# Routing weights broadcast to 128 partitions from SBUF rows instead of from HBM, with four transposes instead of one

## The reference

```python
x = x + 0.5 * ffn(layernorm(x), ...)
x = x + mixer(layernorm(x), ...)     # gated convolution and linear recurrence
x = x + 0.5 * ffn(layernorm(x), ...)
```

```python
scores = sigmoid(tokens @ router_weight.T)
# the best 2 of 4 groups of experts, of these the best 4 experts
topk_w = scores of the chosen / their sum * 2.5
hidden = silu(tokens @ gate_w[e].T) * (tokens @ up_w[e].T)
mixed  = sum over the chosen e of topk_w[e] * (hidden @ down_w[e].T)
shared = (silu(tokens @ shared_gate.T) * (tokens @ shared_up.T)) @ shared_down.T
```

## Time and profile before

| | |
|---|---|
| median of 3 runs | 724.22 us (724.0 to 727.43) |
| profiled execution, its own time | 724.26 us |
| its span in the profile | 722.5 us |
| TensorE busy | 668.6 us (93%) |
| VectorE busy | 580.9 us (80%) |
| GpSimd busy | 480.9 us (67%) |
| ScalarE busy | 420.2 us (58%) |
| DMA moved | 78.84 MB |

### The profile page before, as it was taken

One profiled execution on the slowest core, in us unless ns is written; L12 is line 12 of the kernel. 1 busy time (PEld: TensorE's weight loads), 2 busy tenths in 40 slices (PEclk: granted clock), 3 DMA queues, 4 the chain that ended last, 5 costly groups with the idle time before them and its releaser, 6 DMA issues. The chain is left out here.

```text
span 722.5 us, 10391 instructions
## 1 busy us (share of the span) xinstructions
PE 668.6 (93%) x3016; PEld 524.4 (73%) x3016; DVE 580.9 (80%) x1543; ACT 420.2 (58%) x801; POOL 480.9 (67%) x714
## 2 busy tenths in 40 slices
PE   6589998988987999999999999999999899999996
PEld 5468776776766887767777787776778677777784
DVE  5787797788978788887897969988788887978663
ACT  4446655664665656566566565655665655665553
POOL 1147657765677766777567775777667776686775
PEclk9899999999999999999999999999999999999999
DMA  8492908308373290925719074461907346190550
GB/s 196 99 205 70 198 1 191 62 5 194 70 168 75 57 216 4 198 55 113 154 46 192 15 178 89 105 133 45 216 7 167 85 99 139 41 196 16 126 128 15
DMA packets 59994, 78.84 MB, mean 109 GB/s; under 512 B 7680, under 2 KB 27168, under 8 KB 59936
## 3 DMA queue, kind: packets, MB, share of 16 engines
q1 hardware_dynamic: 59408, 77.91, 49.8%
q10 hardware_dynamic: 528, 0.26, 0.2%
HBM read 75.01 MB, written 3.15 MB: 108 GB/s over the span
## 5 line engine op out<-in xcount | busy, mean ns | idle before, releaser
L479 POOL TENSOR_TENSOR hid_lo<-hid,hid_hi 128x256 fp32r<-128x256 f32 x544 | 392.1, 743 | 200.7 <-ACT hid_hi L576 200.0
L576 ACT ACTIVATE hid_hi<-hid 128x512 fp32r<-128x512 f32 x272 | 170.5, 627 | 118.5 <-DVE hid L725 117.3
L712 DVE TENSOR_TENSOR weighted<-gate_ps,raw 128x512 f32<-128x512 f32 x256 | 175.4, 685 | 68.7 <-ACT gate_ps L568 55.8
L568 ACT ACTIVATE gate_ps<-gate_ps 128x512 f32<-128x512 f32 x256 | 148.6, 580 | 105.5 <-PE gate_ps L982 103.0
L725 DVE TENSOR_TENSOR hid<-weighted,up_ps 128x512 f32<-128x512 f32 x256 | 174.8, 683 | 13.8 <-DVE weighted L712 0.5
L1025 PE MATMUL down_ps<-hid_hi,wt_hi 128*128 128x512 f32 x272 | 108.7, 400 | 6.7 <-ACT ffn_sb L580 6.7
L1028 PE MATMUL down_ps<-hid_lo,wt_hi 128*128 128x512 f32 x272 | 108.2, 398 | 0.8 <-POOL hid_lo L479 0.7
L1026 PE MATMUL down_ps<-hid_hi,wt_lo 128*128 128x512 f32 x272 | 107.9, 397 | 0.0
L980 PE MATMUL up_ps<-xT_hi,wt_hi 128*128 128x512 f32 x187 | 78.1, 417 | 12.5 <-DVE hid L725 12.2
L980 PE MATMUL gate_ps<-xT_hi,wt_hi 128*128 128x512 f32 x187 | 80.6, 431 | 4.1 <-DVE weighted L712 3.9
L982 PE MATMUL gate_ps<-xT_hi,wt_lo 128*128 128x512 f32 x187 | 74.8, 400 | 0.0
(11 more groups left out here) (140 smaller groups left out, 1082.7 us busy)
## 6 DMA issues: line engine op xcount, KB each, us to landing
raw<-wT_hbm SPq DMA_DIRECT2D x64, 640.0 KB, 13.3
raw<-wT_hbm SPq DMA_DIRECT2D x32, 512.0 KB, 7.7
raw<-wT_hbm SPq DMA_DIRECT2D x32, 256.0 KB, 3.9
x_res<-in_L_attn_x SPq DMA_DIRECT2D x8, 256.0 KB, 5.6
out_x<-x SPq DMA_DIRECT2D x8, 256.0 KB, 2.3
x_ln<-in_L_attn_x SPq DMA_DIRECT2D x7, 256.0 KB, 14.1
raw<-in_L_ffn_gate_w SPq DMA_DIRECT2D x4, 256.0 KB, 5.3
raw<-in_L_ffn_up_w SPq DMA_DIRECT2D x4, 256.0 KB, 4.9
```

Of the source, the lines that this page charges most:

```text
L479: last = nc.gpsimd.tensor_tensor(hid_lo[s][:, cols], hid[s][:, cols], hid_hi[s][:, cols].bitcast(F32), ALU.subtract)
L568: nc.scalar.activation(bank[:, :] if j else silu_sb[:, :], bank[:, :], ACT.Silu).then_inc(silu_done, 1)
L576: nc.scalar.activation(hid_hi[s][:, :], hid[s][:, :], ACT.Copy).then_inc(hid_hi_done, 1)
L712: V.tensor_tensor(weighted[j % 2][:, :], gate_ps[n % BANKS][:, :], wb[:, j - 1, :], ALU.mult)\
```

## The change

The store to HBM and its buffer and semaphore are gone. The transposed weights stay in SBUF in another form: `wT` is now [32, 512], one partition for each expert with its 512 weights in a row, and there are two such buffers, used by turns. To get this form, `w_tok` is laid out as tokens by experts, and TensorE makes four transposes, one for each 128 tokens, each giving 32 x 128; ScalarE then copies 32 x 512. SyncE broadcasts each expert's row from its one partition to the 64 partitions of that expert with a transfer of its own: 32 transfers of 128 KB a unit, in the same four chunks with the same waits. The bytes written to `wb` are the same.

```diff
-        wT_hbm = nc.dram_tensor("wT_hbm", [E, BLK], F32, kind="Internal").ap()
-        w_tok = sb("w_tok", [P, E, TT])
-        wT = {k: sb(f"wT{k}", [P, P]) for k in (1, 4)}
+        w_tok = sb("w_tok", [P, TT, E])
+        wT = [sb("wT0", [E, BLK]), sb("wT1", [E, BLK])]
...
                 else:
-                    for loaded in wb_loaded:
-                        sp.wait_ge(loaded, u * 32)
-                sp.dma_start(wT_hbm.rearrange("e (t p) -> (e t) p", t=TT), wT[k][:, :]).then_inc(wT_stored, 16)
-                sp.wait_ge(wT_stored, u * 16 + 16)
+                    for loaded, (lo, hi) in zip(wb_loaded, CHUNKS):
+                        sp.wait_ge(loaded, u * 32 * (hi - lo))
                 for c, (lo, hi) in enumerate(CHUNKS):
                     if u > 0:
                         sp.wait_ge(weighted_done, (u - 1) * NPAIR + hi)
-                    for half in range(2):
-                        rows = wT_hbm.rearrange("(q h) t -> h q t", h=2)[half, lo:hi, :]
-                        sp.dma_start(wb[half * I:half * I + I, lo:hi, :], rows.partition_broadcast(I))\
-                          .then_inc(wb_loaded[c], 16)
+                    for q in range(lo, hi):
+                        for half in range(2):
+                            row = wT[u % 2][2 * q + half:2 * q + half + 1, :]
+                            sp.dma_start(wb[half * I:half * I + I, q, :], row.unsqueeze(1).broadcast_to([1, I, BLK]))\
+                              .then_inc(wb_loaded[c], 16)
...
-                if u > 0:
-                    act.wait_ge(wT_stored, u * 16)
-                nc.scalar.activation(wT[k][:, :], side[:, 0:P], ACT.Copy).then_inc(wT_done[k], 1)
+                if u > 1:
+                    for loaded, (lo, hi) in zip(wb_loaded, CHUNKS):
+                        act.wait_ge(loaded, (u - 1) * 32 * (hi - lo))
+                nc.scalar.activation(wT[u % 2][:, :], side[0:E, :], ACT.Copy).then_inc(wT_done[k], 1)
...
-                dve.wait_ge(wb_loaded[chunk_of(j - 1)], n // NT * 32 + 32)
+                lo, hi = CHUNKS[chunk_of(j - 1)]
+                dve.wait_ge(wb_loaded[chunk_of(j - 1)], (n // NT + 1) * 32 * (hi - lo))
...
-                    st.done(V.scalar_tensor_tensor(w_tok[:, :, :].rearrange("p e t -> p t e"), chosen[:, :, 0:E], SCALE,
+                    st.done(V.scalar_tensor_tensor(w_tok[:, :, :], chosen[:, :, 0:E], SCALE,
...
-                nc.tensor.transpose(side[:, 0:P], w_tok[:, :, :].rearrange("p e t -> p (e t)"), ident[:, :])\
-                  .then_inc(route_transposed[k], 1)
+                for t in range(TT):
+                    last = nc.tensor.transpose(side[0:E, t * P:(t + 1) * P], w_tok[:, t, :], ident[:, :])
+                last.then_inc(route_transposed[k], 1)
```

More of the change, by code:

```diff
@@ L231, in macaron_kernel @@
         w_lo_done = sem("w_lo_done")
-        wT_stored = sem("wT_stored")
         wb_loaded = [sem(f"wb_loaded{c}") for c in range(len(CHUNKS))]
```

## The result

The changed kernel takes 2191.95 us (median of 4 runs, 2191.88 to 2192.03) where the kernel before took 725.03 us beside it: 3.023 times as long, 95% interval 3.017 to 3.028.

What follows compares the result with a forecast made beforehand. TensorE bounds the kernel before; after the change the broadcasts would. First issue 30.5, transfers 1741, gaps 35, late weights 35, x loads about 10, end 27, outside the span 1.8: together 1880 us, range 721 to 2700.

Steps and rivals of the forecast that it cites:

- places of eight neighbouring partitions: SBUF source of the broadcasts: eight partitions share one rate, 218/8 = 27.3 GB/s, so 4.80 us a transfer with all engines there.
- 16 x 32 x 3.40 = 1741: Broadcast time in us: 16 units of 32 transfers at 3.40 us, geometric middle between one place (4.80) and two (2.40).
- nothing holds the engines together within a unit: DMA engines in the broadcasts: one ahead finds the next place free and gets further ahead, so 3.40 us, not 4.80.
- Gaps of 2.3: SyncE between units: one landing and one issue, 2.3 us, 15 times, 35 us.
- Late weights 35: Three units with weights at slots 13, 16 and 14 wait 2, 5 and 3 tiles of some 3.5 us, 35 us.
- The end from the last landing, 27: After the last broadcast lands: five tiles at 3.4 us (17), then 10.3 us from last weighting to end; 27 us.
- The transposes and the removed store: Three transposes more a unit cost TensorE about 5 us in all; dropping the store gains about 5 us; they cancel.
- The signs I named: Profile after: DMA 30 to 50 GB/s, share near 1; TensorE under 45%; VectorE's broadcast wait longest, over 50 us a unit.
- Everything stands at one place: Rival for the broadcasts: engines stay in step at one place, 4.80 us a transfer, 2600 us; chance 0.17.
- No slower than HBM: Rival for the broadcasts: reading one partition costs nothing extra, only small terms count, 719 to 729 us; chance 0.22.
- The engines spread widely: Rival for the broadcasts: three to eight places at work, 1.6 to 0.6 us a transfer, 728 to 1300 us; chance 0.14.
- Slower than a place of eight: Rival for the broadcasts: a single partition gives 13.6 GB/s without spreading, about 5070 us, anything over 2700; chance 0.06.

Runs made afterwards that it cites:

- e4: Kernel before, with its eight broadcasts a unit cut into 32 of one row each, still from HBM: 724.41 us, ratio 0.9987.
- e1: Changed kernel with all transfers reading partition 0, the row of expert 0: 2567.48 us.
- e9: Changed kernel with transfers reading partitions 0 and 4 by turns: 1374.79 us.
- e10: Changed kernel with transfers reading partitions 0 and 2 by turns: 2567.66 us.
- e5: Changed kernel's layout, four transposes and 512-column copy, but with the store to HBM and eight broadcasts of the kernel before: 729.11 us, ratio 1.0052.
- e3: Changed kernel with rows laid out so that eight consecutive transfers read eight different groups of four partitions: 1160.74 us.
- e6: Changed kernel with rows laid out so that four consecutive transfers read four different groups of four partitions, the fifth the first again: 1085.70 us.

## Why the prediction was right

*Direction and mechanism.* I forecast 1880 us with a range of 721 to 2700, and 2192 came. That reading all copies of a row out of one partition is what costs, and that the rate is that of a group of partitions, one eighth of the broadcasts' 218 GB/s, is shown: e4 takes the source alone away and the loss is gone, e1 gives the pure door rate, e9 and e10 tell a group from a partition. I worked with places of eight neighbouring partitions. That is wrong: 0 and 4 lie in different ones. The price of one place, 27.3 GB/s and 4.80 us a transfer, was right all the same (median issue 4.758 us), and in that there is luck: with groups of four the 64 partitions that a broadcast writes would be sixteen, and sixteen times 27.5 is twice the 218 GB/s from which I took the eighth. What makes up the difference, these runs do not show.

*The mis-sized term* is 16 x 32 x 3.40 = 1741. It should have been 16 x 132.4 = 2118, 4.14 us a transfer with the landing of the last included. (132.4 is the usual distance from one unit's first issue to the next; in the last unit it is 132.5 from 2038.40 to 2170.94, where VectorE starts on the last chunk.) The step that failed is "nothing holds the engines together within a unit". Something does: only about four transfers are in flight, and in the changed kernel's order four consecutive rows lie behind one door. An engine that is ahead cannot go further than the newest transfer issued, mostly in the same door. The gain over a pure door is what remains: 2192 against 2567, 15%, where I took 29%. It comes where the transfers in flight straddle two doors. Four issues in a row of the changed kernel (ns, least, median, most; then from when to when they started):

```profile
L408 SPq DMA_DIRECT2D raw<-wT x4: 1727/4404/4772, 352.3 to 366.0; - x4
```

and four of the kernel that reads one row only:

```profile
L408 SPq DMA_DIRECT2D raw<-wT x4: 4764/4855/4923, 396.7 to 411.3; - x4
```

In the changed kernel, from the 13th transfer of a unit on, two issues in four take 4.77 us, one about 4.1 and one about 1.9 in the mean, over and over, with the period of four that the rows behind one door have. With one row, or with rows 0 and 2, no issue behind the first three of a unit took under 4.4 us. That the engines do run ahead within these few transfers is an inference from this; no row shows a single engine.

*The other terms.* First issue 30.5, measured 30.63. Gaps of 2.3: from the last issue's end to the next unit's first issue 11 us pass (151.97 to 163.07), most of them the landing of the last transfers, which is in the 132.4. Late weights 35: from one unit's start to the next it was 135.5 and 144.2 us for the first two late ones and 138.6 for the last, against 132.4, about 21 together. The x loads cost nothing outside the 132.4. The end from the last landing, 27: it took 2190.2 - 2170.9 = 19.3. So 30.6 + 2118 + 21 + 19.3 + 1.8 = 2191. The transposes and the removed store, which I let cancel, are 3.8 us together with the store left in (e5), and drown here.

*The signs I named.* DMA at 33 GB/s with a share of 0.8, TensorE at 37% and VectorE's wait for broadcasts, 93 us a unit, came as said; GpSimd and ScalarE waited as long in all (1668 and 1494 us), but for what comes from VectorE. In every unit VectorE's wait was shortest for the first chunk (9.6 us in the mean), but longest for the third (30.3), not for the fourth (25.9). The granted clock was lower, but 0.5 only in single slices of the page, not in long stretches. The broadcasts' 15.1 us from issue to landing is at the low edge of "tens of us". What SyncE waited for was the queue itself more than landed broadcasts: the wait for the unit's landing was 73.7 us in 15 times, the stalled issues over 1,500 us; I had not seen that the issue would block.

*The rivals.* "Everything stands at one place" (2600) is e1's 2567. The result lies between it and my forecast, a little nearer to the forecast: 375 us below 2567 and 312 above 1880. "No slower than HBM" is refuted by e4 against the changed kernel. Its small terms would have given a loss by the transposes of 3.8 us, less whatever the store is worth, which was not tried alone. "The engines spread widely" did not happen in this order of rows, but with other orders the time does fall into that rival's range (e3, e6). "Slower than a place of eight" is refuted by e1, where one partition alone stays under 2700.

## What to carry to other kernels

A broadcast by DMA reads its source once for every copy, so ask how many doors the source lies behind and not only the destination: 64 copies of a row out of one SBUF partition ran at 28 GB/s, the same copies out of HBM at some 200. If the source has to be in SBUF, lay rows that are read one after another behind different doors: 4, 8 and 16 partitions apart were tried, and 8 apart, four doors by turns, took this kernel from 2192 to 1086 us. Count the transfers in flight before hoping for more. One transfer that reads several rows, as the broadcasts from HBM did, was not tried out of SBUF. Where transfers are far from their limit, cutting them finer cost nothing here and let the first user start earlier; that gave this kernel 0.8%. What the store to HBM costs was not tried alone.

## What the runs showed of the hardware that was not expected

- Reading out of SBUF partitions, about four transfers of 128 KB or 4.7 of 64 KB were in flight; then an issue blocked, 4.758 us in the median where it takes some 0.6 free, and everything behind it on SyncE waited (x_ln 4.76 us). Reading from HBM, six of 256 to 640 KB were in flight without a stall.
- Spreading over more doors than two brings less than the doors would give, and not evenly: 58 GB/s with two doors, 78 with four, 65 with eight. That four are better than eight is not explained.
- TensorE's granted clock fell with its idle time: 0.67 in the mean for the changed kernel, 0.65 in e1, 0.84 with four doors, 0.99 before. It cost little here, since TensorE waited anyway in all but the first 31 and the last 19 us.
